# The three per-node scalings between the first and the second pass: from VectorE to GpSimd

## What is computed

```
u = expmap(agg, x, c)                 # mobius_add(x, k * agg)
h = mobius_matvec(weight, u, c)       # tanh(...) * (u @ W.T) / |u @ W.T|
h = mobius_add(h, b_ball, c)
h_tan = jax.nn.relu(logmap0(h, c))
h = expmap0(h_tan, c)
# mobius_add(x, y) = ((1 + 2xy + y2) * x + (1 - x2) * y) / (1 + 2xy + x2*y2), numbers per node: x2, y2, xy
```

## Time and profile before

| | before |
|---|---|
| median of three runs | 5282.82 us (5278.07 to 5283.91) |
| the profiled execution's own time | 5278.94 us |
| its span | 5277.1 us |
| mean granted TensorE clock | 0.805 |
| busy: TensorE / VectorE / ScalarE / GpSimd | 62% / 65% / 35% / 63% |

### The profile page before, as it was taken

The page is one execution under the profiler, slowest core; times in us unless marked ns, Lnnn a source line. Parts: engine busy times, 40 slices in busy tenths (PEclk is TensorE's granted clock), DMA queues, the critical chain, the costliest instruction groups (busy, mean ns, idle before and its releaser), DMA issues. The chain is left out here.

```text
span 5277.1 us, 59132 instructions
## 1 busy us (share of the span) xinstructions
PE 3291.6 (62%) x11741; PEld 2264.1 (43%) x11741; DVE 3440.5 (65%) x10607; ACT 1850.3 (35%) x4402; POOL 3348.5 (63%) x3529
## 2 busy tenths in 40 slices
PE   3388887888543566566564566656662566666667
PEld 2266665666332333333333344434441344444445
DVE  4299999999994666666667555555557455555555
ACT  0555555555684333333335333333336000000001
POOL 0377777777004777777761777777771677777773
PEclk8599999999776777777877888888886777777788
DMA  2454555554114444444435555555554544444443
GB/s 79 113 132 133 133 133 133 135 133 119 49 35 127 107 107 107 107 107 107 107 86 168 131 134 134 132 131 134 134 132 142 138 114 113 114 113 114 106 107 99
DMA packets 302414, 617.14 MB, mean 117 GB/s; under 512 B 66553, under 2 KB 175093, under 8 KB 302070
## 3 DMA queue, kind: packets, MB, share of 16 engines
q0 software_dynamic: 168960, 467.01, 33.9%
q1 hardware_dynamic: 107766, 117.55, 7.4%
q10 hardware_dynamic: 25344, 28.85, 2.1%
HBM read 560.58 MB, written 52.57 MB: 116 GB/s over the span
## 5 line engine op out<-in xcount | busy, mean ns | idle before, releaser
L457 POOL DMA_INDIRECT X<-table,src_tab x2640 | 2499.3, 947 | 1396.4 <-issue 752.7
L562 PE MATMUL psum<-X,onehot 128*128 128x259 f32 x5280 | 1824.7, 489 | 1001.1 <-ACT onehot L699 326.2
L1106 DVE SCALAR_TENSOR_TENSOR A<-A,same_tab,psum 128x259 f32 x3476 | 1670.4, 481 | 799.9 <-PE psum L562 564.3
L562 PEld LDWEIGHTS psum<-X,onehot 128*128 128x128 f32 x5280 | 1162.3, 239 | 1459.2 <-ACT onehot L699 562.1
L447 POOL DMA_INDIRECT X<-table,src_tab x880 | 836.9, 951 | 348.3 <-issue 251.3
L699 ACT ACTIVATE onehot<-G,zero_col,ecols 128x128 f32<-128x128 bf16 x1760 | 727.0, 481 | 701.0 <-PE psum L562 460.2
L571 PE MATMUL psum<-H,G 128*128 x1760 | 605.4, 431 | 314.2 <-DVE G L1194 195.5
L551 PE MATMUL psum<-X,onehot 128*128 128x259 f32 x1760 | 568.4, 408 | 4.3 <-DVE A L1106 2.2
L571 PEld LDWEIGHTS psum<-H,G 128*128 128x128 f32 x1760 | 326.5, 207 | 491.2 <-issue 451.8
L699 ACT ACTIVATE onehot<-onehot,zero_col,coef 128x128 f32<-128x128 bf16 x880 | 365.8, 481 | 128.3 <-DVE coef L1237 107.0
L1194 DVE SCALAR_TENSOR_TENSOR G<-psum,X 128x257 f32<-128x257 f32 x880 | 365.7, 417 | 64.0 <-DMA X<-table,src_tab 39.7
(11 more groups left out here) (324 smaller groups left out, 2863.4 us busy)
## 6 DMA issues: line engine op xcount, KB each, us to landing
X<-table,src_tab POOLq DMA_INDIRECT x3520, 2.8
plain<-rows_dram SPq DMA_DIRECT2D x110, 256.0 KB, 3.5
plain<-rows_dram ACTq DMA_DIRECT2D x176, 160.0 KB, 3.5
table<-H SPq DMA_DIRECT2D x21, 906.5 KB, 7.7
x_dram<-X SPq DMA_DIRECT2D x21, 896.0 KB, 4.2
X<-x_dram SPq DMA_DIRECT2D x14, 896.0 KB, 11.2
X<-in_x SPq DMA_DIRECT2D x2, 6144.0 KB
table<-H SPq DMA_DIRECT2D x1, 6345.5 KB, 27.2
```

What stands on the lines that cost most here:

```text
L457: pool.indirect_dma_start(ring[:, s % SLOTS, :], None, table, bass.IndirectOffsetOnAxis(src_tab[:, s:s + 1], 0)).then_inc(sem(f"batch_in{s ...
L562: pe.matmul(psum[:, k % ACC_BANKS, 0:W], hots[:, k % HOTS, :], ring[:, k, :], start=True, stop=True).then_inc(sem("used"), 1)
L1106: stt(total, total, same, psum[:, t % ACC_BANKS, 0:W], ALU.mult, ALU.add).then_inc(sem("sum_added"), 1)
```

## The change

The 147 scalings (3 sweeps of 49 blocks) are issued by GpSimd, in its queue between the gathers of layer 0 and the wait for the next table. A new semaphore, `scale_go`, tells it when the numbers are there: 1 before sweep 1, 2 and 3 after `move_3` of the two halves, 4 and 5 after `turn_4`. The `scaled` count that `mix` waits for is now raised by GpSimd. In `turn_4` one more instruction is waited for.

```
--- before.py
+++ after.py
@@ -462,6 +462,16 @@
             pool.memset(A[:, :, :], 0.0).then_inc(sem("sums_zero"), 1)
             pool.wait_ge(sem("table_stored"), 16)
             gathers_layer0()
+
+            def scale(go, b, name):
+
+                if go is not None:
+                    pool.wait_ge(sem("scale_go"), go)
+                pool.tensor_scalar(A[:, b, 0:D], A[:, b, 0:D], col(name)[:, b:b + 1], None, ALU.mult).then_inc(sem("scaled"), 1)
+
+            for go, name in ((1, "om"), (2, "be"), (4, "al")):
+                for b in range(NB):
+                    scale(go if b == 0 else go + 1 if go > 1 and b == HALVES[1][0] else None, b, name)
             for q in range(3):
                 pool.wait_ge(sem("table_stored"), 16 + 16 * OUTER * (q + 1))
                 gathers(q)
@@ -1261,10 +1271,8 @@
             chain(dve.memset(X[:, NB - 1, :], 0.0))
             dve.sem_inc(sem("x_padded"), 1)
 
+            dve.sem_inc(sem("scale_go"), 1)
             chain(ts(col("t0"), A[:, :, AUX3], -1.0, None, ALU.mult))
-
-            def scale(b, name):
-                rows(A, name, b).then_inc(sem("scaled"), 1)
 
             def mix(q, b, other, name):
 
@@ -1347,8 +1356,9 @@
                 mobius(h, "hl", half("y2", h), "xy")
                 ts(half("be", h), hl, -1.0, 1.0, ALU.mult, ALU.add)
                 chain(tt(half("al", h), half("num1", h), rho, ALU.mult))
-                tt(half("be", h), half("be", h), half("inv", h), ALU.mult)
+                chain(tt(half("be", h), half("be", h), half("inv", h), ALU.mult))
                 chain(tt(half("al", h), half("al", h), half("inv", h), ALU.mult))
+                dve.sem_inc(sem("scale_go"), 1)
 
             def log_1(h):
                 dve.wait_ge(sem("squared"), 2 * NB + HALVES[h][1])
@@ -1375,8 +1385,6 @@
                 chain(tt(t1, t1, t2, ALU.mult))
 
             for j in range(NB + 2):
-                if j < NB:
-                    scale(j, "om")
                 if 0 <= j - 1 < NB:
                     mix(0, j - 1, H[:, j - 1, 0:D], "t0")
                 if j >= 2:
@@ -1389,8 +1397,6 @@
                 if j == 41:
                     move_3(0)
             for j in range(NB + 7):
-                if j < NB:
-                    scale(j, "be")
                 if 0 <= j - 1 < NB:
                     mix(1, j - 1, H[:, j - 1, 0:D], "al")
                 if 0 <= j - 6 < NB:
@@ -1413,8 +1419,6 @@
                 if j == 46:
                     turn_4(0)
             for j in range(NB + 2):
-                if j < NB:
-                    scale(j, "al")
                 if 0 <= j - 1 < NB:
                     mix(2, j - 1, wide["bb"], "be")
                 if j >= 2:
```

## The result

The changed kernel takes 5309.23 us (median of five, 5308.45 to 5313.06) against 5282.82 us: ratio 1.0054, interval 1.0041 to 1.0067, 26.4 us slower. The profiled execution took 5310.03 us, its span is 5308.2 us, 31.1 us over the span before, and the mean granted TensorE clock 0.802 against 0.805. One execution of one experiment (e_sem_only) took 8724 us at a granted clock of 0.318; ratios are of the others.

The account below looks back on a forecast made before the run. VectorE was taken to set the pace of the three sweeps, no engine being busy throughout. Sweeps 1 and 3 at +9.6 us each and sweep 2 at -7.1 sum to +12.1; 5278.9 + 12.1 + 3.9 gives 5295 us, range 5250 to 5325.

Parts of the forecast that it names:

- likeliest case: Scalings on GpSimd take 0.42 to 0.55 us and hold VectorE: +5 to +21 us, 5288 to 5304 us, chance 0.38.
- The change touches none of them: Passes over the edges: the change lies only in the three sweeps between the first and second pass.
- what the sweeps lose or gain the launch loses or gains: Everything behind the sweeps starts when they end, so their change in time passes in full to the launch.
- last sign of error: Forecast wrong altogether if the stretch before the second pass's first gather does not move by what the sweeps move.
- The price of a scaling: One GpSimd scaling of 256 numbers: 0.455 us from the affine select; bounds 0.34 us and 0.947 us (a gather).
- The hold: Sweeps: mix or dot can't overlap a GpSimd scaling, costing VectorE its 0.455 us, except beside sweep 2's 0.34 us copy.
- first rival: Nothing is held, mix and dot run beside the scalings: sweeps gain 12.7 + 12.3 + 4.9 = 29.9 us, 5253 us; chance 0.26.
- The sum of the sweeps: Sweeps 1 and 3 lose 9.6 us each, sweep 2 gains 7.1 us at 1.20 us a block: +12.1 us.
- The 58.6 us: Sign to look for in the changed profile: sweep 1 takes about 58.6 us rather than 40 us.
- The second rival: GpSimd's scaling is longer than the affine select says, and held: 5324 us at 0.65 us, more beyond; chance 0.23.
- Running ahead ... leaves the sum: GpSimd scalings issued early move a delay from one sweep to the one before, leaving the +12.1 us unchanged.
- The small edits at nothing: Five scale_go increments cost no engine time, turn_4's extra wait under 0.1 us twice, sweep 1's first scaling some 0.3 us.

Follow-up runs that it names:

- e_sem_only: Kernel before with scale_go raised five times by VectorE and waited for by GpSimd, scalings still on VectorE: ratio 0.9999 (0.9989 to 1.0009).
- e_bias_psum: Changed kernel with the bias of sweep 3 copied once to PSUM and read from there by mix: 5989.83 us, run once.
- e_147_ts: Kernel before plus 147 GpSimd tensor_scalars of 32 x 256 numbers on unused SBUF behind layer 0's gathers: 6015.44 us against 6008.8, run once.
- e_sweep2_tt: Changed kernel with only sweep 2 scaled on GpSimd, as 49 one-block tensor_tensors: 5280.73 us against 5275.17 for the kernel before, ratio 1.0011.
- e_tt7: Changed kernel with GpSimd's scalings as 21 tensor_tensors of seven blocks instead of 147 tensor_scalars: ratio 1.006 (1.0043 to 1.0077) to the kernel before.

## Why the prediction was right, and where it was not

The time came out slower, as forecast, and inside the range (5250 to 5325), but by luck: two errors of opposite sign met. The forecast has 25 us too many for the sweeps and 38 too few for the gathers. The 5309.23 us also lie above the likeliest case's own 5288 to 5304.

- *"The change touches none of them"* (the passes over the edges), and "what the sweeps lose or gain the launch loses or gains": this step failed, and it carries the whole sign. The sweeps gained 13.1 us and the gathers, whose line was not edited, lost 38. I priced GpSimd's queue by what stands in it and never asked whether another instruction could change the price of those that were there. No row of the kernel before could have shown it. The prediction's last sign of error wouldn't have caught it either: from the start of the sweeps to the second pass's first gather it is 10.3 us less (301.7 to 291.4), much as the sweeps moved, and the loss lies outside. Why the gathers get slower stays open. The five programs in which they take 956 ns and more have 49 to 147 tensor_scalars ahead of gathers; the seven others, with none or one there, with memsets or tensor_tensors there or with 147 tensor_scalars behind the last gather, have 948 at most. In the five the gathers ahead of the first scaling are slowed as well.
- *The price of a scaling*: 0.455 us by the affine select, measured 0.912 alone and 1.004 on the mean. The affine select was the wrong neighbour; the far bound of 0.947, the gather, was the near one. The estimate by the Trainium skill (GPSIMD Engine Reference, "Elementwise — side-by-side cycle accounting") of 384 ns is off further; its price for two inputs is nearer: the tensor_tensor's 3.31 us for 1792 numbers is 1.85 ns each, or 2.2 cycles at 1.2 GHz, under the 2.6 cycles that the page states for two inputs.
- *The hold*: there, on the instructions and for the reason that I gave (two SBUF inputs against a GpSimd instruction that reads), so the first rival (nothing is held) is out. But I charged each scaling's whole length. It is 0.21 us of 0.91. The Trainium skill's rule (SBUF — State Buffer, "Who interferes with whom") says the whole instruction: the tensor_tensor's 3.36 us agree, the tensor_scalar's 0.21 don't. Nor is 0.21 a constant: it was 0.16 on the dot in e_bias_psum and 0.12 on VectorE's scaling in e_147_ts, each time what brings VectorE into step with GpSimd. And GpSimd is held too, by 0.18 us in sweep 2, which the prediction left out. What part of a tensor_scalar shuts VectorE out stays open.
- *The sum of the sweeps*: +12.1 expected, -13.1 measured. By step: sweep 1, with 0.40 + 0.34 + 0.21 = 0.95 us a block for 1.195. (The 58.6 us that I named for it is 49 x 1.195 and leaves out the 3.6 us around the blocks; by my own +9.6 it should have been 62.7. It took 52.6.) Sweep 2, at TensorE's floor of 1.09 us, took 70.7 us, 8.4 us less. The first rival had promised 12.3 for it. Sweep 3 gained 4.2.
- *The second rival* (longer and held) had the right length, and at 0.947 us would have asked +84 us. Longer and held in full never came together for a tensor_scalar. What it said of the pace was right: GpSimd's own time decides sweep 1, its scalings stand back to back. But VectorE doesn't wait for `scaled` (1.1 us in all); it is held in the instruction.
- *The likeliest case's bounds*: "held at 0.42 to 0.55 us: +5 to +21" doesn't follow from the sum beside it, which gives 2 x 49 x 0.29 - 49 x 0.05 = +26 at 0.55 and +7 at 0.42. That +26 is also the measured difference is chance: neither the length nor the hold was so.
- *"Running ahead ... leaves the sum"*: wrong. A scaling that runs ahead into sweep 1 meets no copy to hide beside. In e_sweep2_tt this turned -4.3 into +4.3 us.
- *The small edits at nothing*: e_sem_only is at 0.9999, but at a clock where longer gathers are hidden, and its gathers take 3 ns more. At 0.80 no run has these edits alone; e_tt7 and e_sweep2_tt have them and gathers at 947 ns.

## What to carry to other kernels

Before work goes onto an idle stretch of an engine, ask what that engine does in the rest of the program, and compare the mean of its old instructions afterwards: 10 ns on 3520 gathers outweighed 147 instructions taken off the busiest engine. A GpSimd instruction that reads SBUF is best laid beside VectorE's copies out of PSUM or instructions with one input in PSUM, which no run here showed held; a VectorE tensor_scalar with its one input in SBUF was. Its length should be measured, not borrowed from another kind. And say which engine paces the program when a gain is quoted: the same change was 0.5% slower at a granted clock of 0.80 and 0.2% faster at 0.75.

## What was not expected of the hardware

- An indirect gather on GpSimd takes 945 to 948 ns on the mean in seven programs (the later 2640) and 956 to 960 ns in five, from its first instance on; the kernel before and the changed one each keep their figure on different chips. What sorts the programs is open.
- A GpSimd tensor_scalar of 128 x 256 numbers with a number per partition takes 912 ns with VectorE waiting, a tensor_tensor with the number broadcast (e_sweep2_tt) 606 ns at the least (788 at the median beside VectorE). With an immediate and 32 partitions the tensor_scalar takes 884, so the column and the other 96 partitions account for 28 of the 912.
- Beside GpSimd tensor_tensors of 3.36 us, VectorE instructions with two SBUF inputs alternate with them one for one, so one of 0.41 us took 3.39. Beside tensor_scalars both engines fall into step and share the loss: 0.12 to 0.21 us a block on VectorE where it is the one that is held, up to 0.18 us on GpSimd.
